# One weight copy per tile, eight expert numbers per load, later fetches and a turned gate in the first layer's sorted experts

## The reference

```python
def _moe(x, gW, gb, W1, b1, W2, b2):          # 4096 tokens, 8 experts, d=128, f=256
    gates = softmax(xf @ gW + gb)
    top2_scores, top2_idx = top_k(gates, 2)
    w = (one_hot(top2_idx, 8) * top2_scores[..., None]).sum(1)
    h = relu(einsum('nd,edf->enf', xf, W1) + b1)
    y = einsum('enf,efd->end', h, W2) + b2
    return einsum('ne,end->nd', w, y)
...
x1 = _ln(src + attn_out, ln1_g, ln1_b)
g = silu(_ln(x1 + _moe(x1), ln2_g, ln2_b))
x = x + s * g                                 # s: the mixer's output
xn = layernorm(x)                             # opens layer 1; its router reads xn @ Wg
```

## Time and profile before

| | us |
|---|---|
| median of 3 runs | 2114.26 (2110.38 to 2117.44) |
| the profiled execution | 2123.1 |
| its span in the profile | 2121.4 |
| loop over pairs, first up to last down | about 600.8 to 727.0 |
| tail, last down to the saved scores | 727.0 to 828.1 |

### The profile page before, as it was taken

The page is one execution under the profiler, slowest core; times in us unless marked ns, Lnnn a source line. Parts: engine busy times, 40 slices in busy tenths (PEclk is TensorE's granted clock), DMA queues, the critical chain, the costliest instruction groups (busy, mean ns, idle before and its releaser), DMA issues. The chain is left out here.

```text
span 2121.4 us, 47214 instructions
## 1 busy us (share of the span) xinstructions
PE 1856.5 (88%) x17845; PEld 1336.7 (63%) x17845; DVE 1399.5 (66%) x3579; ACT 1075.9 (51%) x2782; POOL 794.9 (37%) x871
## 2 busy tenths in 40 slices
PE   5889999978767756988679999689999999999998
PEld 3656666677657754545465556567777777776665
DVE  4858787657435564566258881268888877777677
ACT  6847777622234333222244474267676767676222
POOL 4059700026621582037552264633333333333000
PEclk9769999979879966999865589899999999999999
DMA  3180110022133313312420024500000000000000
GB/s 117 69 44 2 22 22 2 2 69 48 45 123 99 94 35 108 116 19 38 90 106 2 23 69 100 107 27 1 1 1 2 1 1 2 1 1 2 6 16 20
DMA packets 146191, 87.78 MB, mean 41 GB/s; under 512 B 67984, under 2 KB 139440, under 8 KB 144816
## 3 DMA queue, kind: packets, MB, share of 16 engines
q1 hardware_dynamic: 129888, 67.58, 12.8%
q0 software_dynamic: 15360, 17.06, 4.3%
q10 hardware_dynamic: 720, 0.14, 0.0%
HBM read 46.46 MB, written 38.27 MB: 40 GB/s over the span
## 5 line engine op out<-in xcount | busy, mean ns | idle before, releaser
L3514 POOL TENSOR_TENSOR l_prob<-l_prob,l_total 128x256 f32<-128x256 f32 x128 | 78.4, 612 | 358.4 <-DVE l_total L3753 358.4
L3651 ACT ACTIVATE l_prob<-l_ps,l_neg_max 128x128 f32<-128x128 f32 (+1 forms) x512 | 208.2, 418 | 0.4 <-DVE l_neg_max L3747 0.4
L2241 DVE TENSOR_REDUCE l0a_peak<-l0a_ps 128x2 f32<-128x512 f32 x256 | 167.7, 686 | 59.2 <-PE l0a_ps L2108 57.4
L2198 ACT ACTIVATE l0a_prob<-l0a_pst 128x512 f32<-128x512 f32 x256 | 139.0, 596 | 81.9 <-PE l0a_pst L2113 81.2
L2108 PE MATMUL l0a_ps<-l0a_qk 32*128 32x256 f32 x1024 | 153.3, 415 | 5.9 <-DVE l0a_peak L2241 4.5
L2113 PE MATMUL l0a_pst<-l0a_qk 32*128 32x256 f32 x1024 | 148.6, 406 | 0.2 <-ACT l0a_prob L2198 0.2
L3759 DVE COPY l_prob_t<-l_pt 128x768 f32<-128x768 f32 x128 | 122.5, 957 | 32.8 <-PE l_pt L3581 32.8
L3515 POOL TENSOR_TENSOR l_prob<-l_prob,l_total 128x512 f32<-128x512 f32 x128 | 133.0, 1039 | 0.0
L2108 PEld LDWEIGHTS l0a_ps<-l0a_qk 32*128 32x128 f32 x1024 | 97.2, 192 | 50.2 <-issue 43.4
L3743 DVE TENSOR_TENSOR l_ps<-l_ps,future 128x512 f32<-128x512 f32 x128 | 89.5, 699 | 51.1 <-PE l_ps L3571 51.1
L3581 PE MATMUL l_pt<-ident,l_prob 128*128 128x128 f32 x768 | 104.9, 273 | 0.0
(11 more groups left out here) (585 smaller groups left out, 5015.4 us busy)
## 6 DMA issues: line engine op xcount, KB each, us to landing
l0x_sent<-zero SPq DMA_DIRECT2D x24, 208.0 KB, 3.0
l0x_rows<-l0x_sent SPq DMA_DIRECT2D x39, 128.0 KB, 2.6
l0x_made<-l0x_y SPq DMA_DIRECT2D x39, 128.0 KB, 1.8
l_band<-zero SPq DMA_DIRECT2D x16, 272.0 KB, 5.7
x_tok<-in_x_dram SPq DMA_DIRECT2D x2, 2048.0 KB, 8.4
l0f_w<-in_L_ffn_W_dram SPq DMA_DIRECT2D x4, 1024.0 KB, 8.8
l2f_w<-in_L_ffn_w_dram SPq DMA_DIRECT2D x2, 2048.0 KB, 9.6
l_rows<-l_band SPq DMA_DIRECT2D x16, 256.0 KB, 3.5
```

The costliest lines, as they stand in the source:

```text
L2198: act.activation(prob[:, (n // 2) % 2, 2 * (n % 2) + j, :, :].rearrange("p t s -> p (t s)"), pst[(2 * n + j) % 3][:, :, :].rearrange("p t ...
L2241: dve.tensor_reduce(to, ps[(2 * m + j) % 3][:, :, :], AX.X, ALU.max, negate=True).then_inc(max_ready, 1)
L3651: act.activation(prob[:, m % 4, h, cols], ps[m % 2][:, h, cols], ACT.Exp, bias=neg_max[:, m % 4, h, t:t + 1], accum_out=total[:, m % 4, h, ...
```

## The change

The weights and biases of an expert now lie beside each other in one table of 642 numbers per expert (`l0f_weights`), so that one copy takes both; they are fetched into it in runs of 1 KB. Expert numbers are read eight at a time into two sets of eight registers. ACT takes the relu of seven tiles in eight (of three in four before). SP issues the fetch of x at pair 8 and the small fetches at pair 16. GpSimd makes all eight groups' diagonals in one instruction each, ahead of its wait for the first 20 pairs. In the tail the normalized group is turned by PE, so that gain and shift are per-partition numbers of ACT's one silu instruction, and turned back by PE; DVE's two instructions for gain and shift go. The order of the tail changes on each engine, and GpSimd brings four blocks for each group in place of three.

```diff
@@ copy_weights (DVE)
-                        e = dve.value_load(r.expert[0:1, s, n:n + 1], min_val=0, max_val=r.E - 1)
-                        dve.tensor_copy(w[:, i % RING, j, :, :], weights[:, :, bass.ds(e, 1), :].rearrange("p k o x -> p k (o x)"))
-                        ins = dve.tensor_copy(bias[:, i % RING, j, :], r.biases[:, bass.ds(e, 1), :].rearrange("p o x -> p (o x)"))
+                        if t % AHEAD == 0:
+                            read_experts(t)
+                        ins = dve.tensor_copy(w[:, i % RING, j, :], r.all[:, bass.ds(mine[t], 1), :].rearrange("p o x -> p (o x)"))
+                def read_experts(first):
+                    some = regs[first // AHEAD % 2][:min(AHEAD, r.TILES - first)]
+                    dve.load(some, numbers[0:1, first:first + len(some)])
+                    for n, reg in enumerate(some):
+                        mine[first + n] = dve.snap(reg, min_val=0, max_val=r.E - 1)
@@ by_act
-                return j == 0 or i % 2 == 0
+                return j == 0 or i % 4 != 1
@@ sync
-                sp.dma_start(st.x[:, :, :], x_in).then_inc(x_fetched, 16)
-                for n in range(2):
-                    sp.dma_start(norms[:, n, :], closing[n]).then_inc(x_fetched, 16)
-                sp.wait_ge(blanked, len(blank))
-                for to, what in fetch:
-                    sp.dma_start(to, what).then_inc(fetched, 16)
                 for i in range(PAIRS + 3):
                     if i + RING < PAIRS:
                         load(i + RING)
+                    if i == 8:
+                        sp.dma_start(st.x[:, :, :], x_in).then_inc(x_fetched, 16)
+                        for n in range(2):
+                            sp.dma_start(norms[:, n:n + 1], closing[n][0:1, :].rearrange("o d -> d o")).then_inc(x_fetched, 16)
+                    if i == 16:
+                        sp.wait_ge(blanked, len(blank))
+                        for to, what in fetch:
+                            sp.dma_start(to, what).then_inc(fetched, 16)
@@ tail, tensor
+                def turn_normed(g):
+                    pe.wait_ge(normed, g + 1)
+                    pe.wait_ge(gate_made, g)
+                    for j in range(GB):
+                        ins = pe.transpose(py[1][:, j, :], st.g[:, g * GB + j, :], c.ident[:, :])
+                    ins.then_inc(n_turned, 1)
+                def turn_gate(g):
+                    pe.wait_ge(gate_made, g + 1)
+                    pe.wait_ge(gate_taken, g)
+                    for j in range(GB):
+                        ins = pe.transpose(pt[1][:, j, :], gate_ch[:, g % 2, j * P:(j + 1) * P], c.ident[:, :])
+                    ins.then_inc(norm1.gate_ready, 1)
+                add_up(0)
+                add_up(1)
+                for x in range(-1, GRP + 1):
+                    if x + 1 < GRP:
+                        turn_normed(x + 1)
+                    if x >= 1:
+                        norm1.route(pe, x - 1)
+                    if x + 1 < GRP:
+                        turn_gate(x + 1)
+                    if 0 <= x < GRP:
+                        norm1.turn(pe, x)
+                    if x + 3 < GRP:
+                        add_up(x + 3)
@@ tail, vector
-                spread_weights(0)
-                spread_weights(1)
-                ...
+                for x in range(-1, GRP):
+                    if x + 1 < GRP:
+                        statistics(x + 1)
+                        centring(x + 1)
+                    if x >= 0:
+                        add_mixer(x)
+                        norm1.centre(dve, x)
@@ gpsimd
+                for g in range(GRP):
+                    full = [P, 2, GB, P]
+                    pool.tensor_tensor(diag[:, g, :, :, :], c.ident[:, :].unsqueeze(1).unsqueeze(1).to_broadcast(full),
+                                       r.weight[:, :, group(g)].unsqueeze(3).to_broadcast(full), ALU.mult).then_inc(diag_ready, 1)
                 all_stored(FIRST)
-                for x in range(GRP + 1):
-                    ... root(x), bring 2, norm1.root(x - 1), bring 1
+                for x in range(-1, GRP):
+                    ... root(x + 1), bring 2, norm1.root(x), bring 2
```

More of the change, by code:

```diff
@@ L1053, with flat @@
     EARLY = 52
+    HID = 2 * P
+    SIZE = 2 * HID + HID // P + D
+    def flat(self):
+        return self.all[:, :, :].rearrange("p e n -> p (e n)")
     def __init__(self, mem, sent, made):
@@ L1647, in layers01 @@
         mem = Memory(nc, ctx)
-        w1, w3 = w12[:, 0:U, :], w12[:, U:2 * U, :]
+        w1, w3 = (r.flat()[:, n * U * P:(n + 1) * U * P].rearrange("p (u x) -> p u x", x=P) for n in range(2))
         w2 = mem.sb("l1f_w2", [P, E1 * H1 // P, D])
@@ L1789, in _ @@
                         down(i - 1)
-                for x in range(GRP + 4):
-                    if x < GRP:
-                        add_up(x)
-                    if 0 <= x - 3 < GRP:
-                        norm1.turn(pe, x - 3)
-                    if 0 <= x - 4 < GRP:
-                        norm1.route(pe, x - 4)
+                add_up(0)
[11 more added lines that the diff above has]
+                        add_up(x + 3)
             @block.scalar
@@ L1829, in _, with make_gate @@
                 load_table(act, c, ACT.Silu)
-                for x in range(GRP + 4):
-                    if x < GRP:
-                        normalize(x)
-                    if 0 <= x - 1 < GRP:
-                        act.wait_ge(gained, x)
-                        norm1.open_gate(act, x - 1)
-                    if 0 <= x - 2 < GRP:
-                        norm1.normalize(act, x - 2)
-                    if 0 <= x - 3 < GRP:
-                        norm1.save_ch(act, x - 3)
+                def make_gate(g):
+                    if g == 0:
+                        act.wait_ge(x_fetched, 48)
+                    act.wait_ge(n_turned, g + 1)
+                    act.activation(gate_ch[:, g % 2, :], py[1][:, :, :].rearrange("p j x -> p (j x)"), ACT.Silu, bias=norms[:, 1:2],
+                                   scale=norms[:, 0:1]).then_inc(gate_made, 1)
+                for x in range(-1, GRP + 1):
+                    if x + 1 < GRP:
+                        normalize(x + 1)
+                    if x >= 1:
+                        norm1.save_ch(act, x - 1)
+                    if x + 1 < GRP:
+                        make_gate(x + 1)
+                    if 0 <= x < GRP:
+                        norm1.normalize(act, x)
             @block.vector
@@ L1844, in _ @@
                 spread = [P, GB, D]
+                numbers = r.expert[0:1, :, :].rearrange("p s m -> p (s m)")
+                AHEAD = 8
+                regs = [[dve.alloc_register(f"l0x_e{k}_{n}") for n in range(AHEAD)] for k in range(2)]
+                mine = {}
+                def read_experts(first):
[3 more added lines that the diff above has]
+                        mine[first + n] = dve.snap(reg, min_val=0, max_val=r.E - 1)
                 def copy_weights(i):
@@ L1891, in centring, with add_mixer @@
                     dve.scalar_tensor_tensor(centre[:, g, :], mv[:, g, :, 0], -1.0, rstd[:, g, :], ALU.mult, ALU.mult).then_inc(centre_ready, 1)
-                def scale(g):
-                    dve.wait_ge(normed, g + 1)
-                    n = st.g[:, group(g), :]
-                    link(dve.tensor_tensor(n, n, norms[:, 0, :].unsqueeze(1).to_broadcast(spread), ALU.mult))
-                    dve.tensor_tensor(n, n, norms[:, 1, :].unsqueeze(1).to_broadcast(spread), ALU.add).then_inc(gained, 1)
+                def add_mixer(g):
+                    dve.wait_ge(norm1.gate_ready, g + 1)
+                    product = norm1.gate[:, g % 3, :, :]
+                    dve.tensor_tensor(product, pt[1][:, :, :], st.s[:, group(g), :], ALU.mult).then_inc(gate_taken, 1)
+                    dve.wait_ge(gate_taken, g + 1)
+                    link(dve.tensor_tensor(st.x[:, group(g), :], st.x[:, group(g), :], product, ALU.add))
+                    for j in range(GB):
+                        ins = dve.bn_stats(norm1.stats[:, g, j, :], st.x[:, g * GB + j, :])
+                    link(ins)
+                    for j in range(GB):
+                        ins = dve.bn_aggr(norm1.mv[:, g, j, :], norm1.stats[:, g, j, :])
+                    ins.then_inc(norm1.stats_ready, 1)
                 dve.wait_ge(*ready)
@@ L1909, in _ @@
                 dve.wait_ge(x_fetched, 48)
-                spread_weights(0)
-                spread_weights(1)
-                for x in range(GRP + 3):
-                    if x < GRP:
-                        statistics(x)
-                        centring(x)
-                    if x + 2 < GRP:
-                        spread_weights(x + 2)
-                    if 0 <= x - 1 < GRP:
-                        norm1.statistics(dve, link, x - 1)
-                    if x < GRP:
-                        scale(x)
-                    if 0 <= x - 1 < GRP:
-                        norm1.centre(dve, x - 1)
```

(14 more changed lines are left out.)

58 lines of the change are left out of this document (18 added, 40 removed).

## The result

The changed kernel takes **2080.61 us** (median, 2078.73 to 2085.24) against 2113.99 beside it: ratio 0.9846, 95% interval 0.9822 to 0.9869, 33.4 us less. Forecast were 2071 and 43 us less. The time lies outside the inner band of 2062 to 2078, which had 0.66, and inside the whole range of 2060 to 2090, close to the times of rivals A (2082) and C (2083), neither of whose causes came. Run once more in another series, it gave 0.9853 (0.9829 to 0.9878).

A forecast was written before the change was run, and what follows sets the result against it. VectorE was taken to bound the loop at 2.93 us a pair, TensorE's 2.00 afterwards. First root 42 us earlier plus tail 1 us less gave 43 off the median: 2071 us, inner band 2062 to 2078 (0.66), whole range 2060 to 2090.

The forecast's parts named there:

- Rival A: In the loop, the load of eight numbers is paid per register, 2.5 us; VectorE stays the bound; 2082 us, chance 0.08.
- Rival C: Fetches in mid-loop hold rows back, a stall of 13 us at pair 13 or 21; 2083 us, chance 0.06.
- The diagonals cost GpSimd eight products: Early in the stage, behind GpSimd's last send and blanking: 17 us of products, where GpSimd now waits 65 us.
- rival B: In the loop, denser copies starve GpSimd's fetches, 0.5 us for each of 32, 16 us later; 2087 us, chance 0.07.
- The start gap: At the loop's start, TensorE's 12.79 us idle for rows goes, since load(4) no longer waits behind GpSimd's blanking.
- Copy and load: In the loop, one copy of 642 numbers and one load of eight: VectorE needs 1.8 to 2.3 us a pair.
- x's fetch: With x fetched at pair 8, load(13) lands 0 to 5 us late; 1.5 us taken.
- The clock: Granted clock averages 0.93 while GpSimd fetches; costs TensorE 5 us by the loop's end, 2 by its middle (0 to 9).
- The tail: From the first root to the stage's end: 91.5 to 94.5 us against 93.9; 93 taken, 1 us less.
- The two DVE products that go … bring little: In the tail, VectorE's two removed products ran beside GpSimd's fetches, so removing them brings little.
- D: In the loop, a dense TensorE isn't granted its clock; 3.9 us a pair at half clock; 2136 us, chance 0.02.
- E: A latency (relu to `down`, copy to `up`) holds the loop at 2.5 us a pair; 2089 us, chance 0.08.

The follow-up runs named there:

- kernel 5: The change with GpSimd's eight diagonal products cut into sixteen halves, each waiting for one more pair's weight copies, counted from pair 7 on; ratio 0.9794 to the kernel before.
- 10: The kernel before with only the fetches moved: x and the closing norm at pair 8, the next stage's at pair 16; ratio 0.9943 to the kernel before.
- 9: Kernel 5 with the fetches of x, closing norm and next stage back at the start of SyncE's list, behind the blanking; ratio 0.9843 to the kernel before.
- kernel 2: The change with the diagonals alone undone: VectorE makes them in the tail, GpSimd has no products; ratio 0.9802 to the kernel before.
- kernel 3: The change with the fetch of x and the closing norm's columns at pair 20 instead of pair 8; 2087.12 us, ratio 0.9844 to the kernel before.
- kernel 4: The kernel before with only the diagonals moved to GpSimd, eight products back to back at the phase's start; ratio 1.0011 to the kernel before.
- kernel 1: The change with the diagonal products cut into sixteen halves, each waiting for one more pair's weight copies, from pair 2 on; 2074.69 us, ratio 0.9786 to the kernel before.
- kernel 6: Kernel 5 with products counted from pair 13 on and eight back-to-back GpSimd zero fills of the same areas ahead of them; one execution, 2087.43 us.

## Why the forecast held in direction and missed in size

- **The step that failed**: "The diagonals cost GpSimd eight products … behind its last send", taken at nothing in the sum, with GpSimd's 65 us of idle time as the cover. Their own duration was right, even a little long (1.88 us each against 2.08), and GpSimd did have the time. What I didn't ask is what the engine beside it does meanwhile: VectorE's copy, on which the loop hangs, had to wait for all eight. It cost 15 us between up(7) and up(10) (12.7 of idle, the rest half clock), of which 12.6 are left by up(38) against kernel 5, since it also covered the wait for x; the first root came 12.5 later than forecast. I had the lock in rival B, only in the other direction (copies starving GpSimd), and priced that one alone; the fetches there grew from 1.285 to 1.31 us apart, under 1 us in all.
- In the trace of before GpSimd computed nothing beside a copy of VectorE, and a copy's worst case of 0.62 us was beside fetches. A hint that the two engines meet stood in the tail, though, in the direction in which GpSimd pays (kernel before; VectorE's product by the closing shift, and GpSimd's last root step of the seventh and of the eighth group):

```profile
814.98 0.69 DVE L1897 TENSOR_TENSOR ffn_out<-ffn_out,l0x_norms 128x512 f32<-128x512 f32 x1
815.11 1.45 POOL L245 TENSOR_TENSOR norm_rstd<-norm_rstd,minus_half 128x4 f32<-128x4 f32 x1
...
819.80 1.04 POOL L245 TENSOR_TENSOR norm_rstd<-norm_rstd,minus_half 128x4 f32<-128x4 f32 x1
```

  One and the same step takes 1.45 us beside a product of VectorE and 1.04 with none beside it. An operation that the trace doesn't show beside its neighbours should have been bounded by its whole duration: 17 us, a rival at 2088.
- **Without that step the sum stands**: kernel 5 has the first fetch at 44.8 us (forecast 44.2), the first root at 86.1 (86.2), and 43.6 us of gain by the ratio (43). The agreement in the last number is in part luck: at L298 the trace of kernel 5 stands at 174.9 where the sum gives 179.2 (86.2 and 93), because the tail was too long in it.
- **Two errors partly cancel.** In the change the first root came 12.5 us late and the tail took 4.9 us less than forecast; with the tail as forecast the time would have been near 2085.5.
- **The start gap** (12.8): 13.4 and 14.7 in kernels 10 and 9. **Copy and load**: 1.8 to 2.3 us a pair of VectorE were forecast; four pairs have four times 0.91 us of copies and 0.42 of the sum, one relu of 0.60 and idle times of 1.02 and three of 0.14, about 1.8 a pair. Rival A (a price per register) is false: 0.60 us for eight and not 2.5. **ACT** was covered.
- **x's fetch** (1.5, between 0 and 5): hidden by the stall in the change, waits of 0.79 us (kernel 2) to 2.84 us (kernel 3) where nothing hides it.
- **The clock** (5 us by the loop's end): none; the loop ran at 1.00 beside the fetches, with TensorE busy 60.00 of 60.00 us. Neither the fetches nor TensorE's idle times alone lowered it in the earlier trace rows: kernel 4 has the loop of before, the same fetches and more idle time (TensorE busy 16.98 of 24 us against 18.62), and ran at 1.00 (columns as in the earlier trace rows). What did lower it is open.

```profile
676.00:700.00 24.00, 16.98 (x144) 16.15 (x144) 14.18 (x48) 10.98 (x33) 17.87 (x18) 1.00 0.48 132
```

- For x and the clock together 6.5 us were forecast, and 2.5 came in kernel 5 (74.7 less 36 pairs of 2.005; 2.1 of it at x's wait, most of the rest at the two late relus), so its up(38) is at 74.7 and not at 78.5. That brought nothing, as the text had it of a faster loop: GpSimd's fetches lead to the first root.
- **The tail** (93 us, measured 88.1): the pace of the last groups held (roots 7.1 to 7.2 us apart, forecast 7.14). Two terms were too long: the first four groups took 50.1 us in place of 52 (roots 11.5 and three times 12.9 us apart and not 13.4), and the rest took 38.0, where the sum had 39.4 to 42.4 and took a value in between.
- "The two DVE products that go … bring little" was wrong against the kernel before. There the second norm's two root steps took 0.57 and 1.45 to 1.46 us on GpSimd in seven groups of eight, each beside the scale products of VectorE (two operands from SBUF), and 0.23 and 1.04 in the eighth, where no such product runs; now they take 0.23 to 0.25 and 1.04 in all eight. That is 0.76 us for each of seven groups, 5.3 us, close to the 5.8 by which the tail became shorter; that the one makes the other is argued. The kernels with the old tail (4 and 10) have the same two values, those with the new one the short ones alone. The sum didn't see this gain because its rows (1.56 us at the first norm's root, 4.21 at the last group) were of roots with no such product beside them. No run takes the products out by themselves; that they are the cause rests on the groups with and without them in kernels before, 4 and 10.
- Rival C's 13 us stall didn't come, nor did D's half clock in a loop without idle times (it stood for some 5 us behind the stall alone), nor E's latencies.

## What to carry to other kernels

An idle GpSimd is no free place for work beside VectorE's copies within SBUF: in these kernels a row of its products of two operands, or of its fills, without gaps stopped the copy for the whole row, and small one-operand products were stretched by the copy in their turn. Cut such work and let each piece wait on the copy's own semaphore, with the count chosen by where GpSimd is when it gets there, not by where the row begins. And where a change removes one gap, ask of every other edit whether that gap was its cover.

## What the runs showed of the hardware

- The hold lasts over many instructions: 14.53 us for one copy of 0.50 us, over eight products of GpSimd (1.88 us each); 6.85 us for one copy over eight fills (0.97 us each). The Trainium skill, SBUF — State Buffer, section Who interferes with whom, says of GpSimd and of VectorE's instructions in the modes with two ports that whoever issues first gets the shared ports "for the whole instruction". The traces agree on the direction (the products had begun 0.7 us before the copy), but between the instructions of an unbroken row the copy doesn't get in: it ended 0.35 us after the last of the row in the change, in kernel 1 and in kernel 6.
- 64 tensor-by-column products of 128x128 in a row did not hold the copy (0.98 us at most). They took 0.59 us with no copy beside them and up to 1.25 with one.
- Spaced products cost two copies 0.5 us together (1.40 in place of 0.90) for each product of 1.04 us.
- A load of eight neighbouring numbers into registers takes 0.60 us, one takes 0.31.
- GpSimd's two-operand product takes 1.04 us for 128x512 and 1.88 us for 128x1024.
